# Graph attention over a 64x32 image: softmax operands kept in PSUM, immediate biases, and a new order of a slot

## What is computed

```python
alpha = relu(bn(einsum('bchw,oc->bohw', x, wa)))      # 32 channels
sigma = relu(bn(einsum('bchw,oc->bohw', x, ws)))      # 32 channels
att = einsum('bkn,bkm->bnm', alpha, sigma)
att = softmax(where(adj, att, NEG), axis=2)           # adj: the 8 neighbours of a pixel
h_s = einsum('bnm,bcm->bcn', att, xf)
Gc = einsum('bcn,bdn->bcd', xf, xf)
catt = softmax(where(cadj, Gc, NEG), axis=2)          # cadj: the 2 neighbouring channels
h_p = einsum('bcd,bdn->bcn', catt, xf)
out = (1 - gama) * x + gama * elu(h_s + h_p)
```

## Time and profile before

| | us |
|---|---|
| median of 3 runs | 604.75 (601.31 to 605.41) |
| the profiled execution | 608.46 |
| its span in the trace | 606.7 |
| mean granted TensorE clock | 0.904 |

### The profile page before, as it was taken

How to read it: one execution, slowest core, us unless ns; L and a number is a source line. 1 busy time by engine, 2 the same in 40 slices (tenths; PEclk the granted TensorE clock), 3 DMA queues, 4 the chain that set the end, 5 groups by cost and what they waited for, 6 DMA issues and landing times.

```text
span 606.7 us, 18825 instructions
## 1 busy us (share of the span) xinstructions
PE 492.1 (81%) x7621; PEld 385.8 (64%) x7684; DVE 380.1 (63%) x669; ACT 429.2 (71%) x1043; POOL 233.9 (39%) x140
## 2 busy tenths in 40 slices
PE   0468989888898888979798888989798997888783
PEld 0236677666767575767667575767667686675672
DVE  3213576665857666675857676675857676584872
ACT  0244678758877777858777777868877777787683
POOL 5200044334424442444334442444334442443365
PEclk9995997979899898979999898979999797889877
DMA  8990055765666567655766567655767477523113
GB/s 234 241 244 15 3 169 145 210 191 154 179 190 191 165 188 209 199 168 166 199 179 193 161 200 209 193 178 166 196 190 208 126 210 204 178 87 124 71 71 139
DMA packets 55702, 102.28 MB, mean 169 GB/s; under 512 B 6208, under 2 KB 6464, under 8 KB 55616
## 3 DMA queue, kind: packets, MB, share of 16 engines
q1 hardware_dynamic: 55616, 101.07, 58.0%
HBM read 34.20 MB, written 33.55 MB: 112 GB/s over the span
## 4 chain that ended last, share of the span: by engine, by line
PE 49%; DVE 24%; issue 13%; ACT 12%; DMA 2%; SPq 1%; POOLq 0%; DVEq 0%; ACTq 0%
PE z L439 17%; PE gb L439 13%; DVE z L361 9%; PE xp L449 8%; PE score L439 7%; ACT probs L263 5%; DVE gram_d L385 4%; PE et L525 4%; ACT z L278 3%; DVE neg_max L339 3%; DVE gram_e L380 2%; ACT upper L235 2%; DMA const<-constants_dram 2%; DVE probs_t L354 1%; DVE probs L346 1%
## 5 line engine op out<-in xcount | busy, mean ns | idle before, releaser
L214 POOL TENSOR_TENSOR blend<-elu,blend 128x1024 f32<-128x1024 f32 x64 | 150.8, 2356 | 360.7 <-ACT elu L290 360.7
L439 PEld LDWEIGHTS z<-probs_t,upper 64*128 64x128 f32 x2304 | 165.1, 201 | 76.5 <-issue 75.1
L439 PE MATMUL z<-probs_t,upper 64*128 64x128 f32 (+1 forms) x2304 | 182.6, 295 | 36.1 <-DVE z L361 34.1
L449 PE MATMUL xp<-const,x 128*128 128x128 f32 x512 | 94.9, 314 | 44.7 <-ACT upper L235 37.6
L361 DVE SCALAR_TENSOR_TENSOR z<-near,catt,z 128x512 f32<-128x512 f32 x128 | 91.8, 752 | 61.8 <-ACT z L278 61.7
L263 ACT ACTIVATE probs<-score,neg_max 128x128 f32<-128x128 f32 x256 | 90.5, 371 | 55.2 <-DVE neg_max L339 55.2
L278 ACT ACTIVATE z<-x,vec,catt 128x512 f32<-128x512 f32 x128 | 94.6, 773 | 10.2 <-DVE catt L393 9.9
L235 ACT ACTIVATE upper<-xp 128x512 f32<-128x512 f32 x128 | 76.0, 594 | 32.3 <-PE xp L449 28.4
L449 PEld LDWEIGHTS xp<-const,x 128*128 128x128 f32 x512 | 62.1, 157 | 57.5 <-issue 50.7
L366 DVE SCALAR_TENSOR_TENSOR elu<-elu,z 128x512 f32<-128x512 f32 x128 | 81.8, 680 | 14.7 <-ACT elu L285 14.7
L439 PE MATMUL score<-key,query 32*64 32x64 f32 (+1 forms) x1536 | 78.3, 247 | 13.9 <-issue 5.8
(11 more groups left out here) (49 smaller groups left out, 253.5 us busy)
## 6 DMA issues: line engine op xcount, KB each, us to landing
x<-x_dram SPq DMA_DIRECT2D x64, 512.0 KB, 6.2
out_dram<-blend SPq DMA_DIRECT2D x64, 512.0 KB, 4.1
near<-x SPq DMA_DIRECT2D x128, 224.0 KB, 5.0
near<-x SPq DMA_DIRECT2D x128, 30.0 KB, 4.6
const<-constants_dram SPq DMA_DIRECT2D x1, 435.5 KB, 10.2
const<-constants_dram SPq DMA_DIRECT2D x1, 128.0 KB, 2.1
wt<-w_dram SPq DMA_DIRECT2D x1, 64.0 KB, 3.4
vec<-vectors_dram SPq DMA_DIRECT2D x1, 5.5 KB, 3.1
```

Source lines behind the costliest of these rows:

```text
L214: nc.gpsimd.tensor_tensor(blend[s % BLENDS][:, :, :], elu[s % 2][:, :, :], blend[s % BLENDS][:, :, :], ALU.add).then_inc(blend_done, 1)
L439: return nc.tensor.matmul(o, l, r, start=start, stop=stop, skip_group_check=True, **kw)
L449: last = nc.tensor.transpose(xp[:, v * C + h * P:v * C + (h + 1) * P], xb[:, h, at0:at0 + WIN], ident)
```

## The change

- The exponentials of the scores are written back into the bank `score`, in place, and `normalise` reads them there and writes `probs`. `scores(s)` on PE now waits for `norm_done` of the step before (it waited for `exp_done`), and the wait for `pt_done` moves from ACT's exponentials to DVE's product.
- The side products, the pairs and the exponentials of the channel softmax lie in columns 68 to 79 of the bank `gb` (`SIDES`, `PAIRS`, `POWERS`). One `tensor_copy` of one column is added for `shift_gram`, which still needs `gram` in SBUF. `project_query` waits for `catt_done` instead of `gram_ready`.
- The biases 1.0 and -1.0 are given as numbers.
- The order of a slot changes on ACT, DVE and PE. `project_query`, `project_key` move one quarter earlier (q1 and q2); the key and the edges stand before the second value half, the query behind it.

```diff
+SIDES, PAIRS, POWERS = 68, 72, 76
...
-V_GAMA, V_ONE, V_MINUS = 8, 9, 10
+V_GAMA = 8
...
-        vec = sb("vec", [P, 11])
+        vec = sb("vec", [P, 9])
...
         band = sb("band", [P, 3, BAND])
-        gram = sb("gram", [P, 3])
-        gram_e = sb("gram_e", [P, 2, 2])
+        gram = sb("gram", [P, 1])
         pair_max = sb("pair_max", [P, 2])
         gram_d = sb("gram_d", [P, 2, 2])
-        gram_x = sb("gram_x", [P, 2, 2])
         pair_sum = sb("pair_sum", [P, 2])
         pair_inv = sb("pair_inv", [P, 2])
         catt = sb("catt", [P, 2, 2])
@@ -92,6 +91,8 @@
         score = bank("score")
         et = bank("et")
         gb = bank("gb")
+        pairs = gb[:, PAIRS:PAIRS + 4].rearrange("p (s l) -> p s l", l=2)
+        powers = gb[:, POWERS:POWERS + 4].rearrange("p (s l) -> p s l", l=2)
         z = [[bank(f"z{i}{h}") for h in range(HALF)] for i in range(2)]
...
                 act.wait_ge(max_done, s + 1)
-                if s >= 2:
-                    act.wait_ge(pt_done, s - 1)
                 for v in range(GQ):
-                    last = nc.scalar.activation(probs[s % 2][:, v, :], score[:, v * WIN:(v + 1) * WIN], ACT.Exp,
+                    last = nc.scalar.activation(score[:, v * WIN:(v + 1) * WIN], score[:, v * WIN:(v + 1) * WIN], ACT.Exp,
                                                 bias=neg_max[s % 2][:, v:v + 1], accum_out=row_sum[s % 2][:, v:v + 1])
                 last.then_inc(exp_done, 1)
 
             def exp_gram(b):
                 act.wait_ge(gram_ready, b + 1)
-                nc.scalar.activation(gram_x[:, :, :], gram_d[:, :, :], ACT.Exp).then_inc(gram_exp, 1)
+                nc.scalar.activation(powers, gram_d[:, :, :], ACT.Exp).then_inc(gram_exp, 1)
 
             def weigh_own(s, h):
                 b, q = s // QUARTERS, s % QUARTERS
@@ -276,13 +275,13 @@
                 if s >= 2:
                     act.wait_ge(elu_done, 2 * (s - 2) + h + 1)
                 nc.scalar.activation(z[s % 2][h][:, :], xs[b % XBUFS][:, 1 - h, cols(q)], ACT.Identity,
-                                     scale=catt[:, h, 1 - h:2 - h], bias=vec[:, V_ONE:V_ONE + 1]).then_inc(product_done, 1)
+                                     scale=catt[:, h, 1 - h:2 - h], bias=1.0).then_inc(product_done, 1)
 
             def exp_z(s, h):
                 act.wait_ge(z_done, s + 1)
                 if s >= 2:
                     act.wait_ge(blend_done, s - 1)
-                nc.scalar.activation(elu[s % 2][:, h, :], z[s % 2][h][:, :], ACT.Exp, bias=vec[:, V_MINUS:V_MINUS + 1])\
+                nc.scalar.activation(elu[s % 2][:, h, :], z[s % 2][h][:, :], ACT.Exp, bias=-1.0)\
                     .then_inc(ez_done, 1)
 
             def times_gama(s):
@@ -295,28 +294,28 @@
             act.wait_ge(bn_done, 1)
             for t in slots:
                 b, q = t // QUARTERS, t % QUARTERS
-                if b + 1 < B:
-                    move_xt(b + 1, q, 0)
                 for h in range(HALF):
                     if real(t - 3):
                         exp_z(t - 3, h)
+                if b + 1 < B:
+                    move_xt(b + 1, q, 0)
+                if q == 2 and b + 1 < B:
+                    move_query(b + 1)
+                if q == 3 and b + 1 < B:
+                    move_key(b + 1)
+                if real(t - 3):
+                    times_gama(t - 3)
+                if q == 1 and 0 <= b < B:
+                    exp_gram(b)
                 if real(t):
                     exp_scores(t)
                 if b + 1 < B:
                     move_xt(b + 1, q, 1)
-                if q == 1 and 0 <= b < B:
-                    exp_gram(b)
-                if q == 2 and b + 1 < B:
-                    move_query(b + 1)
                 if q == 3 and b + 1 < B:
-                    move_key(b + 1)
+                    move_halo(b + 1)
                 for h in range(HALF):
                     if real(t - 1):
                         weigh_own(t - 1, h)
-                if real(t - 3):
-                    times_gama(t - 3)
-                if q == 3 and b + 1 < B:
-                    move_halo(b + 1)
 
...
                 dve.wait_ge(exp_done, s + 1)
                 nc.vector.reciprocal(row_inv[s % 2][:, :], row_sum[s % 2][:, :]).then_inc(inv_done, 1)
                 dve.wait_ge(inv_done, s + 1)
-                nc.vector.tensor_tensor(probs[s % 2][:, :, :], probs[s % 2][:, :, :],
+                if s >= 2:
+                    dve.wait_ge(pt_done, s - 1)
+                nc.vector.tensor_tensor(probs[s % 2][:, :, :], score[:, :].rearrange("p (v m) -> p v m", m=WIN),
                                         row_inv[s % 2][:, :].unsqueeze(2).to_broadcast([P, GQ, WIN]),
                                         ALU.mult).then_inc(norm_done, 1)
 
@@ -372,25 +373,24 @@
                                              .rearrange("p (l k) -> p l k", l=3),
                                              gb[:, 0:BAND].unsqueeze(1).to_broadcast([P, 3, BAND]),
                                              ALU.mult))
-                nc.vector.reduce_sum(gram[:, :], band[:, :, :], AX.X).then_inc(gram_side, 1)
+                then(nc.vector.reduce_sum(gb[:, SIDES:SIDES + 3], band[:, :, :], AX.X))
+                nc.vector.tensor_copy(gram[:, :], gb[:, SIDES:SIDES + 1]).then_inc(gram_side, 1)
 
             def gram_softmax_in(b):
-                dve.wait_ge(gram_side, b + 1)
-                flat = gram_e[:, :, :].rearrange("p s l -> p (s l)")
-                nc.vector.tensor_tensor(flat[:, 0:3], gram[:, :], const[:, C_END:C_END + 3], ALU.add)
                 dve.wait_ge(shift_done, b + 1)
-                then(nc.vector.tensor_tensor(flat[:, 3:4], gb[:, SHIFT:SHIFT + 1], const[:, C_END + 3:C_END + 4],
-                                             ALU.add))
-                then(nc.vector.reduce_max(pair_max[:, :], gram_e[:, :, :], AX.X))
-                nc.vector.tensor_tensor(gram_d[:, :, :], gram_e[:, :, :],
+                nc.vector.tensor_tensor(gb[:, PAIRS:PAIRS + 3], gb[:, SIDES:SIDES + 3], const[:, C_END:C_END + 3], ALU.add)
+                then(nc.vector.tensor_tensor(gb[:, PAIRS + 3:PAIRS + 4], gb[:, SHIFT:SHIFT + 1],
+                                             const[:, C_END + 3:C_END + 4], ALU.add))
+                then(nc.vector.reduce_max(pair_max[:, :], pairs, AX.X))
+                nc.vector.tensor_tensor(gram_d[:, :, :], pairs,
                                         pair_max[:, :].unsqueeze(2).to_broadcast([P, 2, 2]),
                                         ALU.subtract).then_inc(gram_ready, 1)
 
             def gram_softmax_out(b):
                 dve.wait_ge(gram_exp, b + 1)
-                then(nc.vector.reduce_sum(pair_sum[:, :], gram_x[:, :, :], AX.X))
+                then(nc.vector.reduce_sum(pair_sum[:, :], powers, AX.X))
                 then(nc.vector.reciprocal(pair_inv[:, :], pair_sum[:, :]))
-                nc.vector.tensor_tensor(catt[:, :, :], gram_x[:, :, :],
+                nc.vector.tensor_tensor(catt[:, :, :], powers,
                                         pair_inv[:, :].unsqueeze(2).to_broadcast([P, 2, 2]),
...
             nc.vector.tensor_tensor(bn[:, 7, :], part[:, 1, :], bn[:, 2, :], ALU.subtract).then_inc(bn_done, 1)
             for t in slots:
                 b, q = t // QUARTERS, t % QUARTERS
+                for h in range(HALF):
+                    if real(t - 3):
+                        elu_out(t - 3, h)
                 if q == 1 and 0 <= b < B:
                     gram_softmax_in(b)
                 if real(t):
                     maxima(t)
-                for h in range(HALF):
-                    if real(t - 3):
-                        elu_out(t - 3, h)
+                if real(t - 1):
+                    move_probs(t - 1)
                 if q == 1 and 0 <= b < B:
                     gram_softmax_out(b)
+                if q == 0 and 0 <= b < B:
+                    gram_pick(b)
                 if real(t):
                     normalise(t)
-                if q == 0 and 0 <= b < B:
-                    gram_pick(b)
-                if real(t - 1):
-                    move_probs(t - 1)
                 for h in range(HALF):
...
                 if b > 0:
-                    pe.wait_ge(gram_ready, b)
+                    pe.wait_ge(catt_done, b)
                 project(b, slice(0, HID), query_done)
 
...
                 if s > 0:
-                    pe.wait_ge(exp_done, s)
+                    pe.wait_ge(norm_done, s)
                 m0 = (q > 0) * WIN + (q == QUARTERS - 1) * WIN
...
                 if real(t - 1):
                     transpose_probs(t - 1)
                 if q == 2 and b + 1 < B:
+                    project_key(b + 1)
+                if q == 3 and b + 1 < B:
+                    edges(b + 1)
+                if real(t - 2):
+                    z_sums(t - 2, 1)
+                if q == 1 and b + 1 < B:
                     if b < 0:
                         pe.wait_ge(const_in, 48)
```

(6 more changed lines are left out.)

3 lines of the change are left out of this document (1 added, 2 removed).

## The result

| kernel | us, median (range) | its profiled execution: us, span, clock |
|---|---|---|
| before | 605.08 (601.31 to 607.01) | 608.46, 606.7, 0.904 |
| after | 587.97 (581.41 to 593.43) | 592.32, 590.5, 0.885 |

The ratio is 0.963, with a 95% interval of 0.955 to 0.972: 3.7% faster. The forecast was 548 us (9.4%), with a range from 525 to 578, and the result lies outside it. Of the four runs of the changed kernel two, the profiled one among them, are over 1.5% slower than its fastest (mean clocks 0.885 and 0.891 against 0.912 and 0.916); the ratio, and every difference between kernels in this document, compares the other runs alone, whose median here is 582.5 us. So the lower clock of the profiled execution is not the change's; but the clock hardly rose either, while every wait that the change aims at has gone.

The account below looks back on a forecast made before the run. TensorE, busy 81%, bounds the kernel: an image of 34.20 us less 3.57 of waits and 1.45 of clock is 29.2, plus 1.1, 0.3 and 0.1 is 30.7. Over the run, with end and median corrections: 548 us, range 525 to 578.

Parts of the forecast that it names:

- the other 1.39 us without work: TensorE's idle time in one 34.20 us image beyond the 3.57 us of waits, taken as issue gaps the change leaves.
- I price the queue at nothing: SP's DMA queue: same DMAs in the same order, stores following an earlier times_gama, so no cost.
- The walk: One image of the new order stepped through ACT, DVE and PE with traced durations: 30.7 us an image.
- The wait for the mix: PE before the value sums of q0, ACT becoming late in q3: 1.1 us, against 0.69 in the kernel before.
- the "even" stretch to the query projection: From the pick in q0 to q1's query projection: DVE 7.3 us against PE 7.4, at most 0.1 lost.
- The two waits of q2: PE before q2's transposes (1.38 us) and value sums (1.50 us), both from q1's late channel softmax; claimed to go.
- Channel softmax: DVE lines 380 and 385 with one SBUF operand each: 0.15 and 0.16 us, taking 2.8 us from DVE an image.
- Biases: Constants in ACT's instruction save 85 to 94 ns, four times a slot, 0.35 us, counting only in q3.
- rival 2: A DVE or ACT chain priced short, 564 us; a bias still read from memory, 553; 0.30 together with rival 1.
- Rival 1: Waits go but the clock stays down in one slot of four: 1.45 us an image, 570 us; 0.30 with rival 2.
- Rival 3: ACT runs ahead into q3, the 1.1 us wait vanishes with the shift wait: 29.2 us an image, 526 us; chance 0.17.
- Rival 4: Scores waiting behind normalise become the loop in every slot, PE at 1.2 GHz: 35.9 us an image, 626 us; chance 0.04.

Follow-up runs that it names:

- burst_late: The changed kernel (`after`) with one more wait on SyncE, so the loads of quarter 0 are issued only when gram_band is done: 536.5 us, ratio 0.886 to before.
- before_soft: The kernel before with only the channel softmax put into PSUM, old order, biases, exponentials and SyncE's program kept: 556.0 us, ratio 0.917 to before.
- late_sbuf_soft: `burst_late` with the channel softmax in SBUF tiles as before, the rest as changed: 547.5 us, ratio 0.906 to before.
- late_vec_bias: `burst_late` with the biases of both z operations read from the tile vec as before: 564.4 us, ratio 0.937 to before.
- late_no_inplace: `burst_late` with the score exponentials written to the SBUF tile as before, not in place: 536.4 us, ratio 0.886 to before.
- s_first: The changed kernel (`after`) with the scores ahead of the value sums in quarter 0 too: 560.0 us, no ratio, runs from 546.7 to 563.6.

## Why the prediction was wrong

**The step that failed** stands in its first paragraph: "the other 1.39 us without work (34.20 - 29.24 - 3.57) are issue gaps that the change does not touch", with its companion "I price the queue at nothing". The stops among these gaps are PE waiting for its own program behind the loads that SP issues. The change moved that burst into the band, so stops of 0.3 to 1.0 us (one of 1.5) became 2.3 to 3.2 in six images, with the clock low for up to 17 us beside them. `after` less `burst_late` is 46 us, and 536.5 lies 12 from the forecast of 548, inside its range. That nearness is in part luck, since the forecast had the gaps and the biases mis-sized.

The reading of the 1.39 us was wrong too. One gap of 0.59 us in that image, at 292.65, is such a stop, 2.5 us after a packet of q8. Four more, 0.69 us together, stand in front of the scores, where the trace of before lacks the record of the mask matmul (the trace of after has all 64): there PE worked. The last is 0.11.

**The walk held.** Four of the images without a stop take 29.7 to 30.0 us (30.7 forecast); two take 31.0 and 32.2, with a fall of the clock. The wait for the mix was 1.39 us (1.1). The wait of `shift_gram` was 0.2 at most, in 5 images (0.3), and the "even" stretch to the query projection lost 1.3 us once, not 0.1 an image. The two waits of q2 are gone. With no stop, PE's busy 28.04 and the wait of 1.39 leave 0.29 us without work, where I had carried 1.39: that term was too high by 1.1, in part because of the missing records, and the wait for the mix too low by 0.3.

**Channel softmax.** 159 and 161 ns, as priced. Its worth depends on the order: some 50 us in the old (`before_soft`), 11 in the new (`late_sbuf_soft`). I credited the waits' removal to it and to the order together and never asked what each gives alone.

**Biases.** The durations were nearly right: 600 and 703 ns against 679 and 773, 70 to 79 ns less where 85 to 94 were priced; in q0 0.32 us measured for 0.35. The term was mis-sized: 5 us forecast in rival 2, 28 measured in `late_vec_bias`, for it left the clock out.

**In place.** Priced at nothing, measured at nothing (`late_no_inplace`); PE waits in front of the scores for 3.3 us in three places. The exponential is even 26 ns shorter than the earlier trace rows have it, 345 for 371.

**The rivals.** Rival 1 named the right consequence (a clock that stays down behind a wait in q0 with the issue gaps beside it) and priced it at 1.45 us an image; measured over 29.7, and with the stop itself, it was 3.7 to 9.4 in the seven images with a stop. It called the gaps given, so its 570 was still too low. Rival 2's slow chain did not come. Rival 3's wait did not vanish by itself; the edit of `s_first` covers it, and with the burst moved that gave 512, below its 526. Rival 4 did not come. No rival asked what the queue's new place would collide with.

**What stays open.** Why a wait of 1.39 us leaves the clock up in most images of `burst_late` and not in all, and how much of the 46 us is the stops' own and how much belongs to falls that began behind that wait. That PE waits for a block's transfer rests on the 66 stops, each 2.3 to 2.9 us behind the start of a packet, and on the shifts of boundary and burst; the request for a block itself is in no record. Nor does a full burst hold every packet back: in `burst_late` 12 of the 61 started with the DMA engines over 90% busy in the microsecond before and in the second one after. And the profile of `after` is of an execution of 592 us, 10 over the 582.5 that its ratio rests on; how long the stops are in the others is not recorded.

## What to carry to other kernels

An idle time that the trace puts down to "issue" has a cause too: compare its place with the instruction queue's packets and with the bulk transfers around it, before calling it untouched. Where a new order moves a burst of DMAs against an engine with many small instructions, try holding the burst back with one wait; here that was worth more than the change. And price a wait of PE by what the clock does behind it, since 0.32 us more of waiting in each image cost 28 us and not 5.

## What the runs showed of the hardware that I had not expected

- TensorE runs dry of its own program. Its instructions come in blocks of 16 KB (61 for some 15,700). Blocks that found the DMA engines idle started 125 to 144 matmuls ahead of their use in `after`, those of the long stops, behind a full burst, 0 to 2; PE goes on 2.3 to 2.9 us after the start. A shift of the block boundary by dead matmuls moves the kernel between 557 and 606 us.
- The clock is sensitive to the length of one wait. After 1.39 us it mostly stayed at 2.4 GHz (`burst_late`, low clock 45.7 us in all), after 1.71 us in the same place it fell to 1.2 GHz in ten of 14 images (`late_vec_bias`, 110.8 us).
- A DVE product of four elements per partition can take 1.3 to 2.4 us when both operands are in SBUF and GpSimd adds at that time, and 0.16 us otherwise.
